# Attention on one core: queries and keys transposed and split by the projection stage, 1024-wide maxima, context kept transposed and divided in the output projection

## What is computed

```python
x = x + _L0_attn_ref(_layernorm(x), Wq, bq, Wk, bk, Wv, bv, Wo, bo)

def _L0_attn_ref(x, Wq, bq, Wk, bk, Wv, bv, Wo, bo):
    q = _rope(proj(Wq, bq)); k = _rope(proj(Wk, bk)); v = proj(Wv, bv)     # (B, 16, T, 16)
    scores = jnp.einsum('bhqd,bhkd->bhqk', q, k) / sqrt(16)
    attn = jax.nn.softmax(scores, axis=-1)
    ctx = jnp.einsum('bhqk,bhkd->bhqd', attn, v)
    return ctx.transpose(0, 2, 1, 3).reshape(B, T, D) @ Wo + bo
```

## Time and profile before

| | us |
|---|---|
| median of 3 runs | 5796.52 |
| lowest, highest | 5791.26, 5796.96 |
| the profiled execution | 5787.34 |
| its span | 5785.5 |

### The profile page before, as it was taken

How to read it: one execution, slowest core, us unless ns; L and a number is a source line. 1 busy time by engine, 2 the same in 40 slices (tenths; PEclk the granted TensorE clock), 3 DMA queues, 4 the chain that set the end, 5 groups by cost and what they waited for, 6 DMA issues and landing times. The chain is left out here.

```text
span 5785.5 us, 90426 instructions
## 1 busy us (share of the span) xinstructions
PE 4965.7 (86%) x30716; PEld 3321.4 (57%) x30716; DVE 3664.5 (63%) x5323; ACT 2335.8 (40%) x3637; POOL 1633.5 (28%) x1327
## 2 busy tenths in 40 slices
PE   6789999999999985399997657675599999988999
PEld 3433333333333344388886324333499999987888
DVE  7878888888888864511111587787576677754443
ACT  1057777777777752022221333332222222223333
POOL 3822222222222211044443144443133233320000
PEclk9979999999999996599998678787699999999999
DMA  5500000000000038133333501011944444445553
GB/s 200 179 14 22 15 22 15 22 22 15 22 17 20 22 107 306 57 56 72 70 61 67 195 29 58 29 58 47 323 102 97 108 99 96 96 101 210 177 182 131
DMA packets 487591, 512.22 MB, mean 89 GB/s; under 512 B 58336, under 2 KB 445408, under 8 KB 478944
## 3 DMA queue, kind: packets, MB, share of 16 engines
q1 hardware_dynamic: 277856, 316.99, 17.1%
q10 hardware_dynamic: 184960, 159.40, 10.6%
q0 software_dynamic: 24576, 33.57, 3.5%
HBM read 291.65 MB, written 218.23 MB: 88 GB/s over the span
## 5 line engine op out<-in xcount | busy, mean ns | idle before, releaser
L662 DVE TENSOR_REDUCE att_mx<-att_s 128x1 f32<-128x512 f32 x2112 | 1306.1, 682 | 145.1 <-PE att_s L542 141.0
L643 ACT ACTIVATE att_pt<-att_sT 128x512 f32<-128x512 f32 x2048 | 1078.8, 598 | 431.0 <-PE att_sT L571 430.9
L542 PE MATMUL att_s<-att_KT,att_QT 96*128 96x512 bf16 x2112 | 821.1, 392 | 28.9 <-DVE att_mx L662 15.3
L571 PE MATMUL att_sT<-att_QT,att_KT 128*128 128x512 bf16 x2048 | 749.4, 384 | 18.1 <-ACT att_pt L643 17.2
L542 PEld LDWEIGHTS att_s<-att_KT,att_QT 96*128 96x128 bf16 x2112 | 206.5, 98 | 620.2 <-DVE att_mx L662 469.3
L1695 POOL TENSOR_TENSOR sl_lg<-sl_lg,sl_sm 128x512 f32<-128x512 f32 x256 | 319.8, 1270 | 844.4 <-DVE sl_sm L1833 844.4
L583 PE MATMUL att_o<-att_pt,att_va 128*32 128x512 f32 x4096 | 544.4, 604 | 6.6 <-DVE att_osb L717 6.6
L1706 PE MATMUL sl_lp<-sl_phi,sl_xT 128*128 (+1 forms) x4160 | 493.1, 277 | 32.6 <-DMA sl_xT<-xnT 23.7
L1706 PEld LDWEIGHTS sl_lp<-sl_phi,sl_xT 128*128 128x128 f32 x4160 | 480.5, 194 | 39.6 <-issue 39.6
L1946 PE MATMUL cb_op<-cb_y,cb_exT 128*128 128x256 f32 x2048 | 485.5, 380 | 0.0
L1160 DVE TENSOR_TENSOR moe_hT<-moe_sg,moe_up 128x512 f32<-128x512 f32 x128 | 88.0, 688 | 619.2 <-PE moe_yp L1097 356.6
(11 more groups left out here) (221 smaller groups left out, 7464.1 us busy)
## 6 DMA issues: line engine op xcount, KB each, us to landing
lg<-sl_raw ACTq DMA_DIRECT2D x128, 512.0 KB, 5.8
cb_ex<-lg SPq DMA_DIRECT2D x64, 1024.0 KB, 6.1
xnT<-n_xnT ACTq DMA_DIRECT2D x64, 512.0 KB, 5.5
n_x<-x SPq DMA_DIRECT2D x27, 1024.0 KB, 10.2
att_gin<-qkv SPq DMA_DIRECT2D x34, 768.0 KB, 5.0
qkv<-qkv_y ACTq DMA_DIRECT2D x64, 384.0 KB, 2.4
xn<-n_xn ACTq DMA_DIRECT2D x24, 1024.0 KB, 9.6
sl_w<-in_L_ffn_W SPq DMA_DIRECT2D x68, 256.0 KB, 3.5
```

What stands on the lines that cost most here:

```text
L542: pe.matmul(s1[:, u % 3, :], QT[par][0:ROWS, h, t * P:(t + 1) * P], KT[par][0:ROWS, h, c * 512:(c + 1) * 512], start=True, stop=True).then ...
L571: pe.matmul(sT[:, idx % 3, :], KT[par][:, h, kt * P:(kt + 1) * P], QT[par][:, h, s // 4 * 512:(s // 4 + 1) * 512], start=True, stop=True). ...
L643: act.activation(pt[:, (s % 2) * HG + h, c], sT[:, k % 3, :], ACT.Exp, scale=HD ** -0.5).then_inc(exp_done, 1)
L662: dve.tensor_reduce(mx2[:, t, h, c:c + 1], s1[:, u % 3, :], AX.X, ALU.max).then_inc(maxed, 1)
```

## The change

The first projection now works on halves of a sequence (512 tokens) with the channels on the partitions: queries and keys come out transposed. There are 32 units: for each of 16 blocks first the queries, then the keys, each of 2 x 128 channels x 512 tokens (the first and the second halves of all heads' values). ScalarE adds the bias; VectorE does the whole rotation; ScalarE and GpSimd split the result into three bf16 parts, which SP stores. The values are made as before, and stored by themselves. In the attention, SP loads the six slots of `QT` and `KT` by 12 DMAs a group, three groups in flight; nothing is split or turned there. The plain scores of 128 queries x 1024 keys are made by two products into two banks and reduced by one instruction: 32 units a group, of which six are made one group further ahead; the transpose of the maxima takes a place in the same row of two PSUM slots. The loops are written out (a list of items for all groups). The context is evacuated by ScalarE alone, twice a group, and stored as it is, transposed, with its denominators beside it. The output projection inverts the denominators, spreads them over 16 partitions each by a product with a 0/1 matrix (`sel`), multiplies the context with them and then with Wo.

```diff
-def qkv_rope(nc, xnT_d, wq, wk, wv, bq, bk, bv, cos_d, sin_d, qkv_d):
+def qkv_rope(nc, xnT_d, wqk_d, bqk_d, wv_d, bv_d, cos_d, sin_d, qk_d, v_d):
...
+                def store(u, part, ready):
+
+                    i, w = u // 2, u % 2
+                    b, t0 = i // HALVES, i % HALVES * N
+                    sp.wait_ge(ready, FLOOR + u + 1)
+                    for two in range(2):
+                        sp.dma_start(qk_d[part, b, w, :, two * 8:two * 8 + 8, t0:t0 + N],
+                                     parts[part][u % NO][:, two, :]).then_inc(stored[u % NO], 16)
...
+                        for two in range(2):
+                            for k in range(KD):
+                                ins = pe.matmul(mm[w][:, two, :], wqk[:, k, 2 * w + two, :], xT[i % 2][:, k, :],
+                                                start=k == 0, stop=k == KD - 1)
+                        ins.then_inc(made, 1)
...
+                add_bias(0)
+                for u in range(UNITS):
+                    if u + 1 < UNITS:
+                        add_bias(u + 1)
+                    round_high(u)
+                    if u >= 1:
+                        round_mid(u - 1)
+                round_mid(UNITS - 1)
...
+                    dve.tensor_tensor(by_cos[u % 2][:], ab[u % 2][:], table(cos, u), ALU.mult).then_inc(cos_ready, 1)
+                    dve.tensor_tensor(by_sin[u % 2][:], ab[u % 2][:], table(sin, u), ALU.mult).then_inc(sin_ready, 1)
...
+                    dve.tensor_tensor(turned[u % NO][:, 0, :], by_cos[j][:, 0, :], by_sin[j][:, 1, :], ALU.subtract)
+                    dve.tensor_tensor(turned[u % NO][:, 1, :], by_sin[j][:, 0, :], by_cos[j][:, 1, :], ALU.add
+                                      ).then_inc(roped, 1)
...
+                def rounded_off(u):
+
+                    pool.wait_ge(hi_ready, FLOOR + u + 1)
+                    if u >= 2:
+                        pool.wait_ge(low_ready, FLOOR + u - 1)
+                    pool.tensor_tensor(rest[u % 2][:], turned[u % NO][:], hi[u % NO][:], ALU.subtract
+                                       ).then_inc(rest_ready, 1)
...
+                for u in range(UNITS):
+                    rounded_off(u)
+                    if u >= 1:
+                        last_part(u - 1)
+                last_part(UNITS - 1)
...
-    UNITS = 2 * HG * NT
+    WIDE = HG * NT
...
+    LEAD, TURN_AT = 6, 2
...
+                def keys_in(n):
+
+                    if n >= NB:
+                        sp.wait_ge(st_done, FLOOR + SINGLES * (n - NB + 1))
+                    b, g = n // G, n % G
+                    for slot in range(S6):
+                        for w, (dst, part) in enumerate(((QT, Q_SLOT), (KT, K_SLOT))):
+                            sp.dma_start(dst[n % NB][slot * HD:(slot + 1) * HD, :, :],
+                                         qk_d[part[slot], b, w, g * HG:(g + 1) * HG, :, :].rearrange("h e t -> e h t")
+                                         ).then_inc(qk_in[n % NB], 16)
...
+                for n in range(NG):
+                    if n >= 1:
+                        context_out(2 * n - 1)
+                        if n + 2 < NG:
+                            keys_in(n + 2)
...
+                        for c in range(2):
+                            ins = pe.matmul(s[i % 2][:, c, :], QT[n % NB][0:ROWS, h, t * P:(t + 1) * P],
+                                            KT[n % NB][0:ROWS, h, c * 512:(c + 1) * 512], start=True, stop=True)
+                    ins.then_inc(scored, 1)
...
+                for g in range(NG):
+                    todo = items_of(g)
+                    for k in range(SINGLES):
+                        score_T(g, k)
+                        if todo and k % 2 == 1:
+                            score(todo.pop(0))
+                            if todo and todo[0][0] == "t":
+                                score(todo.pop(0))
...
+                        if k % (2 * HG) == 2 * HG - 1 and turn >= 4 and turn % 4 == 0:
+                            evacuate(turn // 4 - 1)
...
+                    dve.tensor_reduce(nmx[n % 2][:, t, h:h + 1], s[i % 2][:].rearrange("p c k -> p (c k)"), AX.X, ALU.max,
+                                      negate=True).then_inc(freed, 1)
...
+                def spread_rows(t):
...
+                    for k in range(KD):
+                        ins = pe.matmul(rb[t % 2][:, k, :], sel[:, k, :], rden[:, b, t0:t0 + N], start=True, stop=True)
+                    ins.then_inc(spread_out, 1)
...
+                    dve.tensor_tensor(c[t % U][:], c[t % U][:], rb[t % 2][:], ALU.mult).then_inc(divided, 1)
```

More of the change, by code:

```diff
@@ L278, in _ @@
+                store(UNITS - 1, 1, mid_ready)
+                store(UNITS - 1, 2, low_ready)
+                for j in range(NO):
+                    sp.wait_ge(stored[j], FLOOR + 96 * len(range(j, UNITS, NO)))
+                for j in range(2):
+                    sp.wait_ge(v_stored[j], FLOOR + 16 * (BLOCKS // 2))
             @block.tensor
             def _(pe):
-                def product(t, u, half, loads):
-                    j = u % NB
-                    pe.wait_ge(x_in[half], FLOOR + loads * 16)
-                    tile = slice(u % HT * P, (u % HT + 1) * P)
-                    for n0, n1 in ((0, 512), (512, W)):
+                pe.wait_ge(c_in, FLOOR + 16 * 6)
@@ new lines, in values @@
+                def values(i):
+                    dve.wait_ge(v_made, FLOOR + i + 1)
+                    if i >= 2:
+                        dve.wait_ge(v_stored[i % 2], FLOOR + 16 * (i // 2))
+                    dve.tensor_tensor(v[i % 2][:], vm[i % 2][:], bv[:].rearrange("p (a n) -> p a n", a=1).broadcast_to(
+                        [P, N // P, D]), ALU.add).then_inc(v_ready, 1)
+                dve.wait_ge(c_in, FLOOR + 16 * 6)
+                products(0)
+                for u in range(UNITS):
+                    if u + 1 < UNITS:
+                        products(u + 1)
+                    turn(u)
+                    if u % 2 == 1:
+                        values(u // 2)
@@ new lines, in _ @@
+                pe.wait_ge(identb_ready, FLOOR + 1)
+                for item in items_of(-1):
+                    score(item)
+                pe.wait_ge(ones_ready, FLOOR + NB)
+                before = None
+                for g in range(NG):
[6 more added lines that the diff above has]
+                                score(todo.pop(0))
+                        if k % HG == HG - 1:
+                            if before is not None and before[2] == k // HG % 2:
+                                times_v(*before)
+                                before = (before[0], before[1], 1) if before[2] == 0 else None
+                            if k % (2 * HG) == 2 * HG - 1:
+                                before = (g, k // (2 * HG), 0)
@@ new lines, in _ @@
+                for b in range(B):
+                    dve.wait_ge(den_in[b], FLOOR + 16)
+                    dve.reciprocal(den[:, b, :], den[:, b, :]).then_inc(inverted, 1)
+                divide(0)
+                for t in range(TURNS):
+                    if t + 1 < TURNS:
+                        divide(t + 1)
+                    dve.wait_ge(biased, FLOOR + t + 1)
+                    dve.wait_ge(made, FLOOR + t + 1)
+                    dve.tensor_tensor(x[t % U][:], x[t % U][:], mm[t % 2][:], ALU.add).then_inc(summed, 1)
@@ L821, in _ @@
             @block.gpsimd
             def _(pool):
[L823 to L829 removed]
+                pool.wait_ge(bias_in, FLOOR + 16)
@@ L832, in route @@
+                for t in range(TURNS):
+                    pool.wait_ge(x_in[t % U], FLOOR + 16 * (t // U + 1))
+                    pool.tensor_tensor(x[t % U][:], x[t % U][:],
+                                       bias[:].rearrange("p (a n) -> p a n", a=1).broadcast_to([P, TC, D]),
+                                       ALU.add).then_inc(biased, 1)
 def route(nc, xnT_d, gate_d, ident_d, rowbase_d, idx_d, wt_d):
```

774 lines of the change are left out of this document (354 added, 420 removed).

## The result

The changed kernel takes 5765.14 us, median of five runs (5761.9 to 5768.78), where the kernel before, run beside it, takes 5792.77 (5790.8 to 5796.96). The ratio is 0.9951, 95% interval 0.9936 to 0.9965. That is faster by 0.5%, 28 us, where 151 were forecast; 5765 lies outside the range of 5572 to 5740. It also fell in none of the three rivals: what came belongs to the 0.07 of the others. The profiled execution took 5764.06 us, with a span of 5762.2.

The account below looks back on a forecast made before the run. TensorE's issue with a serial tail was taken to bind the attention loop. Attention -280, first projection +116 and output projection +13 gave -151: 5636 us against the profiled 5787.3, put at 5645 for the runs' median; range 5572 to 5740.

Parts of the forecast that it names:

- the three rivals: Whole program: cheaper engine turns, 5580 us (chance 0.13); 50 us attention groups, 5723 (0.17); late key rows, 6155 (0.08).
- the 0.07 of the others: Whole program: chance 0.07 for outcomes outside forecast and rivals, half of them near or above the old time.
- the three signs of being wrong: Attention groups over 50 us apart, first projection under 260 us, or TensorE waiting on the key rows.
- The order on ScalarE adds a gap: First projection: ScalarE's high part, middle part, then next bias delay VectorE's products, making 8.9 us a unit; lower end 7.8.
- the unit of 8.9 us: First projection: each half block's queries or keys takes 8.9 us, against 5.12 of TensorE; stage 309 us, +116.
- The exclusion of VectorE and GpSimd: First projection: VectorE's two-SBUF-input and GpSimd's SBUF-reading instructions take turns, needing 7.8 us a unit alone.
- the second rival: Attention loop: a group takes 50 us as the fourth-score margin fails and VectorE collides with GpSimd; 5723 us, chance 0.17.
- the first, of cheap turns: First projection: VectorE and GpSimd do not hold each other; ScalarE's loop binds at 6.8 us a unit; 5580 us, chance 0.13.
- the wide maximum that I named: Attention loop: VectorE's wide maximum after the four-operation chain delays TensorE's turn of the maxima, 0.85 us a group.
- the rival that called them late: Attention loop: 12 key-row DMAs pass one after another and TensorE waits, 17 us a group; 6155 us, chance 0.08.
- three trips of 2 us: Output projection start: denominators travel in, out, in, about 2 us each, before the first spread; first store at +19 us.

Follow-up runs that it names:

- e2_load_first: The changed kernel, two token buffers kept, with the load of block i+2's tokens issued ahead of that round's three stores; 5676.22 us, ratio 0.9801.
- e4_psum_operand: The changed kernel with four token buffers, and VectorE's cosine and sine products reading PSUM instead of the biased SBUF copy (bias left out of the result); 5620.07 us.
- e7_no_inversion: The changed kernel without the inversion of the denominators and their way to DRAM and back; spreading and multiplication stay; 5755.52 us, ratio 0.9942.
- e9_turn_back: e3_fused_bias with the low part on VectorE, ScalarE rounding high and middle parts consecutively, and the maxima's turn behind the second early unit; 5583.08 us, ratio 0.9645.
- e3_fused_bias: The changed kernel with four token buffers, VectorE adding the bias and multiplying in one instruction that reads PSUM, without ScalarE's bias pass; 5607.14 us, ratio 0.9681.
- e10_constants_first: e9_turn_back with the loads of the identity and key constants issued ahead of the first group's twelve key loads; 5581.39 us, ratio 0.9643.

## Why the prediction was wrong

The direction was right (faster), the size was not: a gain of 0.5% and not of 2.6%. None of the three signs of being wrong came: no group over 50 us, no first projection under 260 us, no wait on the key rows. They looked for a slower loop and for a shorter first projection; nothing looked for a longer one.

**The first projection is where it failed, at one step.** "If VectorE and GpSimd take turns, they alone need 7.8 us. The order on ScalarE adds a gap ... 8.9 us a unit", and then "31 x 8.9 = 276". Both reasons hold (e2_load_first and e4_psum_operand), and with the token load moved ahead the unit is 8.71 us and the stage 303.3 against the 309 forecast. What is missing is the queue. The prediction counted SP's issues in the attention loop, but never walked SP's own list in this stage, although the change put its 192 stores there (ScalarE's queue had the stores before) and the token load behind them. That load needed its buffer and nothing else, yet waited for the high, middle and low parts, which end the chain that the load before had begun. The step that failed is thus the unit of 8.9 us, in which the wait for tokens was put at nothing without a reason. With two token buffers the loop closes every block: 23.9 us instead of 17.4. Each of the two experiments on it gave 86 to 89 us back, all of the 86 by which the stage missed. The lower clock follows the wait (the granted clock rises from 0.73 to 0.84 when the idling falls from 10.4 to 4.6 us a block) and makes it longer, with 6.6 us for the product inside the loop where 3.4 were forecast. As an estimate from these numbers, 3.2 of the 6.5 us between 23.9 and 17.4 are the clock, and a loop at full clock would still have taken 20.7 us; the two were not run apart.

**The exclusion of VectorE and GpSimd held.** The Trainium skill ("SBUF — State Buffer", Who interferes with whom) spoke for it, and the runs agree: a product of two SBUF operands on VectorE beside GpSimd lasts 3.14 us instead of 1.22, and with one operand in PSUM both engines return to their own times (VectorE 1215 ns, GpSimd 2128 ns), worth 56 us. Where that paragraph of the prediction points to the second rival, the first, of cheap turns, is meant. I fell short on one point, in the expectation for the fused bias: I did not ask which pair would meet next, so it seemed to win 101 us; it won 69.

**The attention loop was right, with two small errors that partly cancel.** The group was forecast at 47.5 us and is 47.8: of the 64 evacuations (now two a group) the first starts at 564.2 and the last group's first at 2047.36, 31 groups apart.

```profile
L692 ACT ACTIVATE att_osb<-att_o x64: 597/597/598, 564.2 to 2064.0; 128x512 f32<-128x512 f32 x64
```
```profile
2047.36 0.60 ACT L692 ACTIVATE att_osb<-att_o 128x512 f32<-128x512 f32 x1
```

The earlier trace rows had 55.3 us a group. The steps between batches with V show the terms. A plain half step is 2.89 us where 2.85 were counted, 46.2 a group for 45.6. A step with an evacuation of the context is 3.02, so the two of a group cost 0.3 us where 0.6 were put down:

```profile
1024.91 1.06 PE L658 MATMUL att_o<-att_pt,att_va 128*32 128x512 f32 x8
1027.80 1.07 PE L658 MATMUL att_o<-att_pt,att_va 128*32 128x512 f32 x8
```

The turn of the maxima waits 0.78 us where I wrote 0.85, against the wide maximum that I named:

```profile
1005.63 2.35 DVE L715 TENSOR_REDUCE att_nmx<-att_s 128x1 f32<-128x1024 f32 x2
...
1006.90 0.45 PE L622 MATMUL att_s<-att_identb,att_naug 128*32 128x128 bf16 x5 [0.78 <-DVE att_nmx L715]
```

The list of TensorE's waits from 600 to 1800 us has none for the key rows. They land 6.8 and 7.3 us (medians) after their issue, twelve of them overlapping, with a DMA share of 0.30; the rival that called them late did not come. Three small sizes were off. The loop's length is 1488.7 us where 31 groups of 47.5 gave 1472.5, +16. The last group with the stores took 48.6 instead of 41, some 5 us of it up to the last evacuation and 3 behind it: its half step is not 1.97 but 2.45 us, since ScalarE's four exponentials (2.06) and the first score behind them (0.39) wait for each other when no plain score stands between:

```profile
2050.31 2.07 ACT L701 ACTIVATE att_pt<-att_sT 128x512 f32<-128x512 f32 x4 [0.39 <-PE att_sT L644]
...
2052.76 2.06 ACT L701 ACTIVATE att_pt<-att_sT 128x512 f32<-128x512 f32 x4 [0.39 <-PE att_sT L644]
```

And the start, up to the first score at 488.34, took 15.8 us instead of 12, while the rest of the fill came out at 47 us for 48. Together +26.

**The output projection was mis-sized by 14 us.** Its first store came 2100.7 - 2072.6 = 28.1 us into the stage instead of 19, +9, and its turns take 81.3 / 15 = 5.42 us instead of 5.15, +4:

```profile
L846 ACTq DMA_DIRECT2D x<-pj_x x16: 378/378/412, 2100.7 to 2182.0; - x16
```

The first spreading product starts 14.2 us into the stage, where three trips of 2 us were allowed. The inversion and its two trips are only 4.4 of these: in e7_no_inversion, with one trip left, it still starts 2077.3 - 2067.5 = 9.8 us after the stage's first load. TensorE, idle until then, spreads at its lower clock, which I had not priced (the granted clock is 0.50 from 2086.8 to 2094.0 us, 0.68 from 2094.0 to 2099.3 and 1.00 from 2101 to 2105):

```profile
2086.83 7.16 PE L822 MATMUL pj_rb<-pj_rden,pj_sel 16*128 16x512 f32 x8 [22.94 <-DMA pj_rden<-rden]
...
2093.92 5.40 PE L835 MATMUL pj_mm<-pj_w,pj_c 128*128 128x256 f32 x16
...
2101.15 3.72 PE L835 MATMUL pj_mm<-pj_w,pj_c 128*128 128x256 f32 x16
```

Eight spreading products take 7.16 us and the first turn's products 5.40, where the next turn's take 3.72. Nor was TensorE over 90% busy there; it was 93.8 of 114.9 us, 82%.

So the sum, in the order of the forecast: attention -253 for -280, first projection +202 for +116, output projection +27 for +13. The change's own idea, wide maxima and no work between transposed scores, did what it should. What it cost in front was nearly ten times what it need cost: with four token buffers, the bias fused into products that read PSUM, and the low part on VectorE (e9_turn_back), the first projection takes 213.8 us, 21 more than before, and the kernel 5583 us, 3.6% faster than the kernel before:

```profile
77.50:291.30 213.80, 171.48 (x512) 97.29 (x512) 177.69 (x240) 68.81 (x65) 71.22 (x34) 0.95 0.71 207
```

## What to carry to other kernels

When a change moves DMAs, write out the queue that receives them as one more engine: for each load ask which entry stands ahead of it and what that entry waits for. A prefetch behind the stores of the work it is meant to run ahead of is no prefetch, and here a deeper buffer and two lines in another order repaired it equally. When naming the signs of being wrong, name one on each side of every term. And when a wait is taken away at one point, look for the next user of the same stream or the same pair of engines, which may hand you the wait back: the fused bias gave two thirds of its price, the later turn of the maxima none.

## What the runs showed of the hardware

- A product of 1024 columns from two SBUF operands on VectorE takes 1.22 us alone and 3.14 beside a GpSimd subtraction of SBUF tiles; the subtraction takes 2.12 alone and 3.18 when VectorE's issues first. With VectorE's first operand in PSUM the subtraction took 2128 ns and the product with the sine 1215, medians of 32 (e4_psum_operand).
- `scalar_tensor_tensor` of 512 columns, (PSUM + bias) x SBUF table, takes 735 ns (median in e3_fused_bias), against 1225 ns for 1024 columns of a plain product: the fused form costs 0.25 us more per 1024 columns and saves ScalarE's pass of 1.25.
- Twelve loads of 128 KB over 16 partitions each, issued 0.47 us apart and followed at once by those of two more groups, hold the first score of the attention until 15.8 us after the first of them is issued in the changed kernel, 16.6 in e9_turn_back, and 15.2 in e10_constants_first, where the small constants go ahead of them.
